# The first unit of each MLP layer as a plain product, with the Strassen-Winograd sums made on VectorE beside it

## What is computed

```python
attn_out = jnp.einsum('btT,bTd->btd', attn, v) @ Wp + bp
target_embed = jax.nn.one_hot(target_codes, V, dtype=x.dtype)[:, None, :]
cms_out = jax.nn.gelu(attn_out @ cW1 + cb1, approximate=False) @ cW2 + cb2
cms_out = cms_out + target_embed
concat = jnp.concatenate([attn_out, cms_out], axis=-1)
modifier = jax.nn.gelu(concat @ mW1 + mb1, approximate=False) @ mW2 + mb2
out = jnp.clip(x + cms_out + modifier, 0.0, 1.0)
```

## Time and profile before

| | |
|---|---|
| median of 3 runs | 2267.79 us (2266.28 to 2269.09) |
| the profiled execution | 2267.46 us, span 2265.2 |
| TensorE busy | 2149.1 us, 95% |
| VectorE busy | 1463.0 us, 65% |
| ScalarE busy | 871.0 us, 38% |
| GpSimd busy | 445.9 us, 20% |
| granted TensorE clock, mean | 0.982 of 2.4 GHz |

### The profile page before, as it was taken

How to read it: one execution, slowest core, us unless ns; L and a number is a source line. 1 busy time by engine, 2 the same in 40 slices (tenths; PEclk the granted TensorE clock), 3 DMA queues, 4 the chain that set the end, 5 groups by cost and what they waited for, 6 DMA issues and landing times.

```text
span 2265.2 us, 28343 instructions
## 1 busy us (share of the span) xinstructions
PE 2149.1 (95%) x10016; PEld 1783.3 (79%) x10016; DVE 1463.0 (65%) x2275; ACT 871.0 (38%) x1494; POOL 445.9 (20%) x404
## 2 busy tenths in 40 slices
PE   8989989999989999999998998999999899899996
PEld 7868768888877877888877886888888688688885
DVE  5577766556567776555666777556566777755564
ACT  4444433333344444332334444333334444433331
POOL 0021121110411113110231112111031212211104
PEclk9999999999999999999998999999999999999998
DMA  7101111114411121111730112111262011111134
GB/s 302 71 29 56 56 56 66 62 50 158 115 64 47 47 70 42 59 63 47 257 97 28 48 49 67 56 65 66 79 182 89 27 48 56 58 52 64 57 107 131
DMA packets 44842, 178.05 MB, mean 79 GB/s; under 512 B 5794, under 2 KB 9890, under 8 KB 37538
## 3 DMA queue, kind: packets, MB, share of 16 engines
q1 hardware_dynamic: 44706, 176.24, 24.1%
HBM read 159.45 MB, written 16.78 MB: 78 GB/s over the span
## 4 chain that ended last, share of the span: by engine, by line
PE 78%; DVE 8%; issue 4%; DMA 4%; ACT 3%; POOL 2%; SPq 1%; ACTq 0%; DVEq 0%; POOLq 0%
PE psum L454 73%; DMA rolep<-roles_in 2%; PE psum L643 2%; DVE cop L951 1%; DVE aop L951 1%; DMA raw_d<-down_in 1%; PE psum L677 1%; PE psum L523 1%; POOL yt L437 1%; POOL yt L439 1%; DVE acc L1109 1%; DVE xs L951 1%; ACT zt L850 1%; DVE stats L1226 0%; SPq L283 0%
## 5 line engine op out<-in xcount | busy, mean ns | idle before, releaser
L454 PE MATMUL psum<-hs,wd 128*128 128x512 f32 x3072 | 722.0, 391 | 2.8 <-DVE hs L951 2.8
L454 PEld LDWEIGHTS psum<-hs,wd 128*128 128x128 f32 x3072 | 580.3, 189 | 126.0 <-DVE hs L951 4.5
L1109 DVE TENSOR_TENSOR acc<-psum,acc 128x512 f32<-128x512 f32 x480 | 312.7, 682 | 127.4 <-PE psum L454 127.1
L454 PE MATMUL psum<-cop,wsm 128*128 128x512 f32 x1344 | 347.7, 395 | 19.0 <-DVE cop L951 19.0
L454 PE MATMUL psum<-aop,wsm 128*128 128x512 f32 x1344 | 347.3, 395 | 18.4 <-DVE wsm L951 11.1
L454 PE MATMUL psum<-aop,wsc 128*128 128x512 f32 x1344 | 329.9, 399 | 34.9 <-DVE aop L951 15.9
L454 PEld LDWEIGHTS psum<-aop,wsc 128*128 128x128 f32 x1344 | 256.8, 193 | 97.8 <-issue 36.0
L454 PEld LDWEIGHTS psum<-cop,wsm 128*128 128x128 f32 x1344 | 255.5, 191 | 75.7 <-DVE cop L951 22.4
L454 PEld LDWEIGHTS psum<-aop,wsm 128*128 128x128 f32 x1344 | 254.2, 190 | 76.9 <-DVE wsm L951 12.8
L951 DVE TENSOR_TENSOR hs<-zt,hs 128x512 fp32r<-128x512 f32 x256 | 175.7, 686 | 92.9 <-ACT zt L850 92.9
L849 ACT ACTIVATE hs<-zt,bias 128x512 fp32r<-128x512 f32 x192 | 137.7, 717 | 247.4 <-DVE zt L1094 168.4
(11 more groups left out here) (118 smaller groups left out, 2531.3 us busy)
## 6 DMA issues: line engine op xcount, KB each, us to landing
w1m<-m_in SPq DMA_DIRECT2D x32, 1024.0 KB, 4.9
rolep<-roles_in SPq DMA_DIRECT2D x64, 384.0 KB, 4.6
w1c<-c_in SPq DMA_DIRECT2D x32, 512.0 KB, 3.6
w<-c_in SPq DMA_DIRECT2D x32, 512.0 KB, 3.6
w<-m_in SPq DMA_DIRECT2D x32, 512.0 KB, 3.6
fw<-fused SPq DMA_DIRECT2D x6, 2048.0 KB, 11.0
fused<-fw SPq DMA_DIRECT2D x4, 2048.0 KB, 6.9
fraw<-fuse_in SPq DMA_DIRECT2D x6, 1024.0 KB, 10.7
```

What stands on the lines that cost most here:

```text
L454: mm = nc.tensor.matmul(out, lhs(a), rhs(b), start=(start and n == 0), stop=(stop and n == total - 1), skip_group_check=reopened)
L1109: nc.vector.tensor_tensor(dst, d_out[o][:, :], dst, ALU.add).then_inc(acc_done, 1)
```

## The change

Unit 0 and unit 8 (`plain(u)`: u is a multiple of 8) are multiplied plainly. `block_products` makes each of the four quadrants from two products of token blocks and weight blocks as they were loaded, 12 matmuls per quadrant and operand set: 48 in unit 0, 96 in unit 8. The four weight blocks use the slots of P6, P7, P4 and P3. The quadrants have a PSUM bank each (2 to 5 in unit 0; 0, 6, 1 and 7 in unit 8), so that the GELU reads PSUM directly. The block x12 gets a pair of parts of its own: for `aop` in the slot of P4 of `cop`, for `cop` in the slot of its P7.

The four differences of token blocks are all made on VectorE (`difference`), each into the low-part memory of its own operand (`aop_raw`, `cop_raw`), which the low part then overwrites in place. `tdiff`, `t1` and GpSimd's `differences` go. The Strassen-Winograd units begin with unit 1 and unit 9; GpSimd combines weights for 14 units per pass, not 16, and unit 0 has four weight blocks to split in the attention, not seven. Some semaphores that counted single transfers are merged. The rest of the order of a unit stays.

```diff
+PLAIN = {(0, 0): P6, (0, 1): P7, (1, 0): P4, (1, 1): P3}
+PLAIN_ORDER = (P6, P7, P4, P3)
+QUADS = (H00, H10, H01, H11)
...
+            def block_products(p, u, h, which, last):
+
+                n, kind = UNITS * p + u, kind_of(u)
+                m, b = h_place(h)
+                ops = cop if which else aop
+                if which == 0:
+                    if kind == 0:
+                        pe.wait_ge(a_sum, 16 * p + 9 + QUADS.index(h))
...
+                for k in range(2):
+                    pe.wait_ge(s_lo[PLAIN[m, k]], n + 1)
+                    if b == 0:
+                        pe.wait_ge(op_lo[(P1, P2)[k]], 2 * p + which + 1)
+                    elif k:
+                        pe.wait_ge(op_lo[P3], 2 * p + which + 1)
+                    else:
+                        pe.wait_ge(x12_lo, 2 * p + which + 1)
...
+                mm = product(plain_bank(kind)[h][:, :], [
+                    (lambda a, k=k, c=c: slot(u, PLAIN[m, k])[:, a, (2 * which + c) * P:(2 * which + c + 1) * P],
+                     lambda a, k=k, c=c: tokens(k)[:, a, c, :], None) for k in range(2) for c in range(2)],
+                    which == 0, last)
...
             def mlps(p):
-                pe.wait_ge(a_sum, 16 * (p + 1))
-                terms(p, 0, P1, P5, P2, P6, P7, P4, P3)
+                for h in QUADS:
+                    block_products(p, 0, h, 0, True)
...
                     else:
-                        for i in (P1, P5, P6):
-                            term(p, u, i, 0, False)
+                        for h in (H00, H10):
+                            block_products(p, u, h, 0, False)
                         down(p, u - 1, 0)
                         down(p, u - 1, 1)
-                        for i in (P1, P5):
-                            term(p, u, i, 1, True)
-                        terms(p, u, P2)
-                        term(p, u, P6, 1, True)
-                        terms(p, u, P7, P4, P3)
+                        for h in (H01, H11):
+                            block_products(p, u, h, 0, False)
+                        for h in QUADS:
+                            block_products(p, u, h, 1, True)
...
-            def differences(p, kind):
...
+                left = {P5: x_block(0, 1), P6: x_block(1, 1), P7: x_block(1, 1), P4: x_block(1, 0)}[i]
+                right = {P5: x_block(0, 0), P6: op_source(kind, P5), P7: x_block(0, 1), P4: op_source(kind, P6)}[i]
+                nc.vector.tensor_tensor(op_source(kind, i), left, right, ALU.subtract).then_inc(t_made[i], 1)
...
-                    for i in (P1, P5, P2) + ((P6,) if u + 1 != NG else ()):
-                        if u + 1 < UNITS:
-                            weight_part(p, u + 1, i)
...
+                    for i in (P6, P7) if u + 1 == NG else (P1, P5, P2, P6) if nxt else ():
+                        weight_part(p, u + 1, i)
...
+                    down_part(p, u)
+                    if nxt:
+                        weight_part(p, u + 1, P4 if u + 1 == NG else P7)
```

More of the change, by code:

```diff
@@ L242, in x_block, with op_source, x12, plain_bank @@
             return acc[:, 2 * k:2 * k + 2, b * TB:(b + 1) * TB]
-        def op_source(i):
-            return {P1: x_block(0, 0), P2: x_block(1, 0), P3: x_block(1, 1), P5: t1[:, :, :],
-                    P7: tdiff[:, 0, :, :], P6: tdiff[:, 1, :, :], P4: tdiff[:, 2, :, :]}[i]
+        def op_source(kind, i):
+            if i in (P1, P2, P3):
+                return {P1: x_block(0, 0), P2: x_block(1, 0), P3: x_block(1, 1)}[i]
+            return (cop_raw if kind else aop_raw)[:, i, LO, :, :]
+        def x12(kind):
+            return cop[:, P7 if kind else P4, :, :, :]
+        def plain_bank(kind):
+            return {H00: ps[0], H10: ps[6], H01: ps[1], H11: ps[7]} if kind else {H00: ps[2], H10: ps[3], H01: ps[4], H11: ps[5]}
         def h_place(h):
@@ L418, in _ @@
                     nc.gpsimd.memset(pblk, 0.0).then_inc(p_zeroed, 1)
[L419 to L424, removed]
+                    for u in range(UNITS):
+                        if not plain(u):
+                            combine(p, u)
                     for s in range(2):
@@ L594, in down @@
                         pe.wait_ge(d_lo, n + 1)
+                    if u == 0 and b == 0:
+                        pe.wait_ge(h_hi[QUADS[o]], n + 1)
                     heres = ((H00, H10), (H01, H11))[b]
@@ new lines, in first_unit @@
+            def first_unit(p, layer, kind):
+                u = NG * kind
+                if kind:
+                    weight_part(p, u, P3)
+                    op_part(p, 1, P1)
+                    op_part(p, 1, P2)
+                x12_part(p, kind)
+                op_part(p, kind, P3)
+                if kind:
+                    down_part(p, u)
+                weight_part(p, u + 1, P1)
+                weight_part(p, u + 1, P5)
+                op_part(p, kind, P5)
+                hidden(p, layer, u, H00)
+                op_part(p, kind, P6)
+                hidden(p, layer, u, H10)
+                weight_part(p, u + 1, P2)
+                weight_part(p, u + 1, P6)
+                op_part(p, kind, P4)
+                hidden(p, layer, u, H01)
+                hidden(p, layer, u, H11)
+                op_part(p, kind, P7)
+                weight_part(p, u + 1, P7)
@@ L1123, in add_x, with first_unit @@
                                                in1=xp[:, :], op0=ALU.add, op1=ALU.add).then_inc(xadd_done, 1)
+            def first_unit(p, layer, kind):
+                u = NG * kind
+                if kind:
+                    weight_part(p, u, P3)
+                    add(p, layer, u - 1, 0, 0, 1, 2, 3)
+                    op_part(p, 1, P1)
+                    op_part(p, 1, P2)
+                    add(p, layer, u - 1, 1, 0, 1, 2)
+                    x12_part(p, 1)
+                    add(p, layer, u - 1, 1, 3)
+                else:
+                    x12_part(p, 0)
+                op_part(p, kind, P3)
+                if kind:
+                    down_part(p, u)
+                difference(p, kind, P5)
+                difference(p, kind, P6)
+                weight_part(p, u + 1, P1)
+                weight_part(p, u + 1, P5)
+                op_part(p, kind, P5)
+                hidden(p, u, H00)
+                difference(p, kind, P4)
+                op_part(p, kind, P6)
+                hidden(p, u, H10)
+                weight_part(p, u + 1, P2)
+                weight_part(p, u + 1, P6)
+                op_part(p, kind, P4)
+                hidden(p, u, H01)
+                difference(p, kind, P7)
+                hidden(p, u, H11)
+                op_part(p, kind, P7)
+                weight_part(p, u + 1, P7)
+                if kind:
+                    add_x(p, layer, u)
```

321 lines of the change are left out of this document (160 added, 161 removed).

## The result

The changed kernel takes 2197.72 us (median of 4, 2193.77 to 2199.93), the kernel before 2268.36 beside it. The ratio is 0.9688 with a 95% interval of 0.9671 to 0.9705: 3.1% less time. The forecast was 2198.

A forecast was written before the change was run, and what follows sets the result against it. TensorE, busy in 95% of the span, bounds the kernel through its matmul count and its waits. Savings of 43.6 us at Place A and 26.1 at B sum to 69.7, from 2267.79 to 2198 us; range 2186 to 2215.

The forecast's parts named there:

- Added work: Units 0 and 8: 18 more matmuls per pass, 72 in all at 0.2267 us, 16.3 us more on TensorE.
- Place A: Start of the MLPs, after the attention, in each pass: 15.3 us each, 43.6 us less over four.
- the wait of 0.5 at unit 1's P6: Start of the MLPs: TensorE waits 0.5 us for P6's operand and weights, bounds 0 and 2 us.
- GpSimd's two short sums: Before unit 1's P6: GpSimd's two remaining weight sums partly block VectorE and hold it up by 0.9 us.
- The wait that stays at B: Before quadrant H10 of unit 8: TensorE still waits for weights P4 and P3, 3.7 us counted in starts.
- B: Change from c weights to m weights (unit 8), each pass: 38.1 us each, 26.1 us less over four.
- unit 9's P6: After unit 8's quadrants: VectorE has its parts ready near 317.2, TensorE asks at 320.6, a slack of 3.4 us.
- The low clock behind it: After the wait before H10: the clock's fall costs 1.75 us per pass, bounds 0 and 3.5.
- The sums on VectorE at no cost: Two 128x1024 subtractions per place, 16 in all at 1.21 us, move to VectorE inside the chain already counted.
- Slower: Rival: in-place differences and splits run at the blocked 3.15 us, not 1.21; 109 us lost, 2307 us; chance 0.03.
- operands still late: Rival: GpSimd and VectorE collide before P6, TensorE waits some 4 us and the clock falls; 2221 us; chance 0.13.
- The prediction's sign, 1.2 to 1.3: Sign of being right: the splits of aop and cop take 1.2 to 1.3 us in the profile after.

The follow-up runs named there:

- e5: The changed kernel with unit 0's quadrant H11 multiplied twice into the same bank, 12 more matmuls per pass: 2208.02 us.
- e9: The changed kernel with three more 128x1024 VectorE subtractions ahead of the difference for P5 at each place: 2214.89 us.
- e4: The changed kernel with unit 8's weight part P3 split before unit 7's last hidden parts on ScalarE and before z21 and z12 on VectorE: 2175.97 us.
- e7: The changed kernel measured and profiled again, nothing altered: 2197.67 us.
- e3: The changed kernel with the differences for P4 and P7 put back on GpSimd, still in place: 2203.63 us.
- e8: The kernel of e3 run again, beside the changed kernel on the same chip: 2198.67 us.
- e1: The kernel before with all four differences of token blocks made on VectorE, products Strassen-Winograd everywhere: 2232.85 us.
- e2: The changed kernel with unit 0 plain but unit 8 back to seven products, all differences on VectorE in place: 2210.58 us.
- e6: The changed kernel with unit 0's first quadrant H00 made to wait for the splits of x12 and P3: 2220.63 us.

## Why the prediction was right, step by step

- **Added work**, 72 matmuls at 0.2267, 16.3 us: right. e5 measured 10.3 for 48, and 2.72 for 12 in its trace.
- **Place A**, 15.3 us per pass: measured 14.92. The step with an error is the wait of 0.5 at unit 1's P6: the split of P6's weights ended at 126.18 in pass 0, not at 127.2, and TensorE asked at 126.6. VectorE's chain began at 114.55 and not at 115.0. And GpSimd's two short sums took nothing from it, where I gave them 0.9: at the first it was GpSimd that was held up (1.65 us at 120.15), and the second began at 125.92, while the last split of the chain ran, and held up only the split behind it (1.77 us at 126.10). The gain was 45.1 and not 43.6. That the chain is tight there was right: e9 found less than 1 us of slack.
- **The wait that stays at B**, 3.7 us in starts: right, 3.58 of idle in all four passes, and for P3's weights. e4 shows that it was one 128x512 part in the wrong place. Behind it nothing waited, as forecast, but the tightest point was not unit 9's P6, where I counted 3.4 us of slack: the last Gelu of unit 8 ends at 306.23, 1.25 us before unit 9's P5 asks at 307.48, and in e9 it came late.
- **The low clock behind it**, 1.75 us per pass: right in kind, and in the first profile too small. The 84 matmuls from H10 to H11 take 20.73, 21.84, 21.72 and 20.78 us in the four passes, against 19.04 at full clock: 1.7, 2.8, 2.7 and 1.7. The 8.9 in sum against the 7.0 forecast are 1.9 us of the missing 2.0 at B (24.1 gained, 26.1 forecast). But the same kernel in e7 loses 0.1, 2.8, 1.7 and 1.7 us behind the same wait, 6.3 in sum, and gains 26.7 at B. So the row of before that showed 1.75 in all four passes gave a fair mean, and that a longer wait costs more is not shown. At A the forecast was 1.5 us too low, at B 2.0 too high in the first profile and 0.6 too low in the second: that the median hits 2198 within 0.3 us is partly luck, the sizes of the terms within 2 us are not.
- **The sums on VectorE at no cost**: right in the total, and e3 with e8 shows that with the plain units it hardly matters who makes them. What the prediction didn't see is how much the sums on GpSimd had cost before: e1 gets half the gain from their move alone, and at B nearly all of it. By counting waits at each place, and not causes, it needed no split between the two, so this did not hurt the number.
- **Slower, or operands still late**: neither came. No 128x1024 split stands in the way of a long GpSimd sum any more; those of `aop` from raw differences average 1.36 us, those of `cop` 1.50. The prediction's sign, 1.2 to 1.3, was a little low.

## What to carry to other kernels

Where the sums of a fast matrix product start a stage, work on the untransformed blocks can fill the time in which the transforms are made; it pays while the added matmuls cost less than the waits they cover (16.3 against some 86 us here, waits and low clock together). Before taking such a step, look at what the operands really wait for: moving two sums off GpSimd gave half the gain and cost nothing on TensorE. Then price the step again, place by place, on top of the cheap one: the plain unit brought 29.2 us more at A, but at B only 2 to 5 for its 48 added matmuls. Behind every wait count also the stretch at the low clock, and try the order of the instructions in front of it: one weight part moved ahead of four VectorE instructions brought another 21.7 us.

## What the runs showed of the hardware

What an idle time costs behind it, by TensorE's clock, is not a fixed price. The changed kernel ran twice under the profiler, and its wait at B in pass 0 is the same both times. The second time (e7):

```profile
272.64 3.00 PE L473 MATMUL psum<-aop,wsm 128*128 128x512 f32 x12 [3.59 <-DVE wsm L1034]
275.48 11.04 PE L473 MATMUL psum<-hs,wd 128*128 128x512 f32 x48
```

Here the granted clock stays at 1.00 (2.4 GHz) from 272 to 278, and the 12 matmuls take 3.00 us; in the first profile they take 4.43, and in pass 1 of both they take 5.46 at 0.50 (1.2 GHz). Time lost behind the same wait, against 0.2267 us per matmul (54 of them in the first three rows, 84 in the others), in the four passes:

| kernel | idle, us | lost behind it, us |
|---|---|---|
| before | 2.78 | 1.8, 1.7, 1.7, 1.8 |
| e1 | 2.78 | 1.7, 0.1, 1.5, 1.7 |
| e2 | 2.78 or 2.79 | 1.8, 0.2, 3.0, 0.1 |
| changed | 3.58 or 3.59 | 1.7, 2.8, 2.7, 1.7 |
| changed, again (e7) | 3.58 or 3.59 | 0.1, 2.8, 1.7, 1.7 |
| e3 | 3.58 or 3.59 | 1.7, 2.9, 0.1, 1.7 |
| e5 | 3.58 to 3.62 | 1.7, 1.6, 3.0, 3.0 |
| e6 | 3.59 or 3.68 | 0.1, 2.6, 1.5, 0.1 |
| e8 | 3.58 to 3.67 | 2.9, 0.1, 1.7, 1.7 |
| e9 | 3.58 | 1.7, 1.7, 1.7, 1.7 |

Shorter waits show the same: 2.03 us before the first row of place A is followed by 6 matmuls in 1.65 us in pass 1 of the kernel before, and by 6 in 2.93 in pass 2 after 2.02 us. In e9 two waits of 1.17 and 1.41 us, 4.4 us apart in starts, cost nothing at the clock behind them in any pass. At B alone this moves the time of one kernel by 2.6 us from one execution to the next (8.9 against 6.3), which is more than some of the effects above.
